# Attention 1 of a two-layer kernel: transposed probabilities by head, values in two passes

## What is computed

```
q, k, v = (x @ W.T).reshape(B, T, 16, 16).transpose(0, 2, 1, 3)   # for Wq, Wk, Wv
scores = einsum('bhqd,bhkd->bhqk', q, k) * 16 ** -0.5, causal mask
attn = softmax(scores)
out = einsum('bhqk,bhkd->bhqd', attn, v).reshape(B, T, 256) @ Wo.T
```

## Time and profile before

| what | us |
|---|---|
| median of three runs | 939.19 |
| lowest and highest run | 936.19, 939.78 |
| the profiled execution, its own time | 939.04 |
| its span, first to last instruction | 937.1 |
| TensorE busy over the span | 863.4 (92%) |
| VectorE busy | 616.3 (66%) |
| ScalarE busy | 567.0 (61%) |
| GpSimd busy | 456.4 (49%) |
| the first attention, from its first matmul to its end | 19.4 to about 178 |

### The profile page before, as it was taken

One profiled execution on the slowest core, in us unless ns is written; L12 is line 12 of the kernel. 1 busy time (PEld: TensorE's weight loads), 2 busy tenths in 40 slices (PEclk: granted clock), 3 DMA queues, 4 the chain that ended last, 5 costly groups with the idle time before them and its releaser, 6 DMA issues. The chain is left out here.

```text
span 937.1 us, 18767 instructions
## 1 busy us (share of the span) xinstructions
PE 863.4 (92%) x6108; PEld 799.0 (85%) x6108; DVE 616.3 (66%) x1620; ACT 567.0 (61%) x1570; POOL 456.4 (49%) x486
## 2 busy tenths in 40 slices
PE   5799997769999999999999999969999999999994
PEld 4699987668989989999889999858888888888884
DVE  5466768667787788877887777664545545454456
ACT  6889888656767776667676676654334343333333
POOL 3734334277677776677677777610222212222121
PEclk9999999998999999999999999997999999999997
DMA  7000000051124111411111111101433333333321
GB/s 238 1 22 27 22 23 1 23 147 35 34 61 122 47 40 40 136 46 45 36 35 46 45 37 47 41 1 41 150 107 102 116 117 100 112 101 117 118 79 45
DMA packets 50246, 63.34 MB, mean 68 GB/s; under 512 B 5728, under 2 KB 36064, under 8 KB 50176
## 3 DMA queue, kind: packets, MB, share of 16 engines
q1 hardware_dynamic: 49088, 61.41, 22.4%
q10 hardware_dynamic: 1088, 1.05, 0.3%
HBM read 41.86 MB, written 1.18 MB: 46 GB/s over the span
## 5 line engine op out<-in xcount | busy, mean ns | idle before, releaser
L639 POOL TENSOR_TENSOR b_prob<-b_prob,b_rsum 128x256 f32<-128x256 f32 (+1 forms) x128 | 104.8, 840 | 104.3 <-DVE b_rsum L621 104.3
L73 PE MATMUL banks<-act_t,b_w 128*128 128x256 f32 (+1 forms) x392 | 129.5, 330 | 4.4 <-DVE b_work L1203 3.3
L74 PE MATMUL banks<-act_t,b_w 128*128 128x256 f32 (+1 forms) x392 | 127.4, 325 | 0.0
L75 PE MATMUL banks<-act_t,b_w 128*128 128x256 f32 (+1 forms) x392 | 127.1, 324 | 0.0
L1965 ACT ACTIVATE moe_hid<-banks 128x512 fp32r<-128x512 f32 x66 | 39.5, 598 | 124.6 <-DVE banks L2056 124.6
L1364 ACT ACTIVATE b_prob<-banks,b_negmax 128x128 f32<-128x128 f32 (+1 forms) x256 | 103.6, 416 | 12.6 <-DVE b_negmax L1351 12.5
L2049 DVE TENSOR_TENSOR moe_gated<-banks,moe_share 128x512 f32<-128x512 f32 x66 | 45.6, 691 | 85.1 <-PE banks L75 81.2
L1220 ACT ACTIVATE b_qt<-b_work 128x512 fp32r<-128x512 f32 x64 | 40.5, 632 | 97.5 <-POOL b_work L1215 97.5
L1215 POOL TENSOR_TENSOR b_work<-b_work 128x512 f32<-128x512 f32 x64 | 88.1, 1377 | 9.2
L639 POOL TENSOR_TENSOR a_prob<-a_prob,a_rsum 128x256 f32<-128x256 f32 x64 | 52.4, 840 | 75.5 <-DVE a_rsum L621 75.3
L1211 POOL TENSOR_TENSOR b_work<-b_work,rope_t 128x512 f32<-128x512 f32 x64 | 83.2, 1299 | 7.2 <-DMA b_work<-b_work 7.2
(11 more groups left out here) (237 smaller groups left out, 3019.1 us busy)
## 6 DMA issues: line engine op xcount, KB each, us to landing
b_work<-b_work SPq DMA_DIRECT2D x128, 128.0 KB, 2.3
moe_share<-gates SPq DMA_DIRECT2D x32, 512.0 KB, 3.6
b_w_raw<-in_b_wq SPq DMA_DIRECT2D x4, 1024.0 KB, 5.5
b_w_raw<-in_b_wo SPq DMA_DIRECT2D x4, 1024.0 KB, 9.0
a_src_t<-act_t SPq DMA_DIRECT2D x5, 512.0 KB, 3.0
moe_w_raw<-in_wg SPq DMA_DIRECT2D x16, 128.0 KB, 2.1
moe_w_raw<-in_wu SPq DMA_DIRECT2D x16, 128.0 KB, 2.2
moe_w_raw<-in_wd SPq DMA_DIRECT2D x16, 128.0 KB, 2.2
```

The source lines that it names most:

```text
L73: nc.tensor.matmul(out, w_lo, m_hi, start=start, stop=False, skip_group_check=skip)
L74: nc.tensor.matmul(out, w_hi, m_lo, start=False, stop=False, skip_group_check=skip)
L75: return nc.tensor.matmul(out, w_hi, m_hi, start=False, stop=stop, skip_group_check=skip)
L639: last = self.m.nc.gpsimd.tensor_tensor(rows, rows, rsum[:, :, t:t + 1].to_broadcast([PART, 2, width]), ALU.mult)
```

## The change

`AttentionA` gets its own versions of four steps and of VectorE's slot.

- **A bank for each head.** Head h's three turned blocks (384 columns, `PCOLS`) lie in one bank of its own. TensorE waits for the low part of the same head of the pair before, turns three blocks, and signals; then it does the same for the other head. The semaphores count heads (`TURNS = 2`).
- **Copied and subtracted by head.** ScalarE makes two copies of 384 columns in place of one of 768, each after its head's turns. VectorE makes two subtractions of 384.
- **By turns.** VectorE's order is maxima of head 0, low part of head 0, maxima of head 1, low part of head 1; then as before.
- **Values in two passes.** A head's block of 128 values' columns holds its high part in 16 columns and its low part in the 16 beside them. One pass over the low and one over the high part of the probabilities does all products: 8 matmuls a pair in place of 12. Four heads fill 128 partitions, so the iteration's output takes 512 columns in place of 256 (two groups, `VG`). The blocks `self.v` need half the room, and GpSimd clears half.
- **Output.** The copy and the subtraction of the output take 512 columns in place of 256. The projection does 12 matmuls in place of 6: two groups, each with weights `wo` in which every head's 16 rows stand twice (for the high and the low part).
- **Weights spread.** At the start of the stage SP issues 16 DMAs from SBUF to SBUF that write the rows of Wo into `wo`, ahead of its first source copy. TensorE waits for them once, before the values of the last pair of iteration 0.

```diff
 class AttentionA(Attention):
+    TURNS = 2
+    def turned(self, h):
+        return self.m.pt_ps[:, 2 * h * SEQ:2 * h * SEQ + PCOLS]
+    def pe_prob_t(self, pe, p, P):
+        wait(pe, self.prob_ready, P + 1)
+        for h in range(2):
+            wait(pe, self.pt_ready, 2 * P - 1 + h)
+            for k in range(PCOLS // PART):
+                last = nc.tensor.transpose(self.turned(h)[:, k * PART:(k + 1) * PART],
+                                           self.prob[:, p, h, k * PART:(k + 1) * PART], m.ident[:])
+            last.then_inc(self.pt_full, 1)
+    def act_prob_t(self, act, p, P):
+        wait(act, self.pv_done, P - 1)
+        for h in range(2):
+            wait(act, self.pt_full, 2 * P + 1 + h)
+            self.m.nc.scalar.activation(self.prob_t_of(p, 0, h), self.turned(h),
+                                        ACT.Copy).then_inc(self.pt_hi, 1)
+    def dve_prob_t(self, dve, p, P, h):
+        wait(dve, self.pt_hi, 2 * P + 1 + h)
+        self.m.nc.vector.tensor_tensor(self.prob_t_of(p, 1, h), self.turned(h),
+                                       self.prob_t_of(p, 0, h).bitcast(F32),
+                                       ALU.subtract).then_inc(self.pt_ready, 1)
+    def slot_dve(self, dve, it, p, units=True):
+        now, prob = self.stage(it, p, 0), self.stage(it, p, 3)
+        for h in range(2):
+            if now:
+                self.dve_max(dve, *now[1:], heads=(h,))
+            if prob:
+                self.dve_prob_t(dve, *prob[1:], h)
...
-        self.v = place(2 * NTT * HPI * PART, "p (a t h n) -> p a t h n", a=2, t=NTT, h=HPI)
+        self.v = place(NTT * HPI * PART, "p (t h n) -> p t h n", t=NTT, h=HPI)
-        self.ot = sb("ot", [PART, 2, SEQ], F32R)
+        self.ot = sb("ot", [PART, 2, VG * SEQ], F32R)
+        self.wo = place(2 * NC * VG * D, "p (a c g n) -> p a c g n", a=2, c=NC, g=VG)
...
     def pe_values(self, pe, it, p, P):
-        wait(pe, self.pt_ready, P + 1)
+        if isinstance(it, int) and it == 0 and p == PAIRS - 1:
+            wait(pe, self.wo_spread, 16 * SPREADS)
         for h in range(2):
             head = 2 * p + h
+            wait(pe, self.pt_ready, 2 * P + 1 + h)
             for k in range(NTT):
-                last = three(nc, m.o_ps[:, k * PART:SEQ],
-                             self.v[:, 0, k, head, :], self.v[:, 1, k, head, :],
-                             self.prob_t[:, par, 0, at:at + width], self.prob_t[:, par, 1, at:at + width],
-                             head == 0 and k == 0, head == HPI - 1 and k == NTT - 1)
+                for part in (1, 0):
+                    last = nc.tensor.matmul(m.o_ps[:, g * SEQ + k * PART:(g + 1) * SEQ], self.v[:, k, head, :],
+                                            self.prob_t[:, par, part, at:at + width],
...
+    def sp_spread(self, sp):
+        src = self.m.a_wo[:].rearrange("p (a c n) -> p a c n", a=2, c=NC).bitcast(F32)
+        for g in range(VG):
+            for h in range(VH):
+                of = (g * VH + h) * A_DH
+                for part in range(2):
+                    to = (2 * h + part) * A_DH
+                    sp.dma_start(self.wo[to:to + A_DH, :, :, g, :].bitcast(F32), src[of:of + A_DH, :, :, :],
+                                 ).then_inc(self.wo_spread, 16)
...
     def pe_project(self, pe, it, p, P):
         for t in range(NTT):
-            last = three(nc, m.y_ps[:, t * D:(t + 1) * D],
-                         self.ot[:, 0, t * PART:(t + 1) * PART], self.ot[:, 1, t * PART:(t + 1) * PART],
-                         m.a_wo[:, bass.ds(at, D)], m.a_wo[:, bass.ds(at + NC * D, D)], True, True)
+            for g in range(VG):
+                o = lambda part: self.ot[:, part, g * SEQ + t * PART:g * SEQ + (t + 1) * PART]
+                last = three(nc, m.y_ps[:, t * D:(t + 1) * D], o(0), o(1), self.wo_at(it, 0, g),
+                             self.wo_at(it, 1, g), g == 0, g == VG - 1)
...
-        self.m.nc.scalar.activation(self.ot[:, 0, :], self.m.o_ps[:, 0:SEQ],
+        self.m.nc.scalar.activation(self.ot[:, 0, :], self.m.o_ps[:],
-        self.m.nc.vector.tensor_tensor(self.ot[:, 1, :], self.m.o_ps[:, 0:SEQ],
+        self.m.nc.vector.tensor_tensor(self.ot[:, 1, :], self.m.o_ps[:],
...
         def _(sp):
+            self.sp_spread(sp)
```

More of the change, by code:

```diff
@@ L318, in _ @@
             nc.gpsimd.memset(m.q_stack[:, 0:NTT * HPI * PART].bitcast(F32), 0.0)
-            k_at = 2 * B_W + 2 * NTT * HPI * PART
+            k_at = 2 * B_W + NTT * HPI * PART
             nc.gpsimd.memset(m.b_w[:, k_at:k_at + NTT * HPI * STACK].bitcast(F32), 0.0)
@@ L423 @@
     LATE_NEXT = False
+    TURNS = 1
     POOL_NORMALISES = False
@@ L566, in act_exp @@
         nc, m = self.m.nc, self.m
-        wait(act, self.pt_full, P - PAIRS + 1)
+        wait(act, self.pt_full, self.TURNS * (P - PAIRS + 1))
         for h in range(2):
@@ L603, in slot_act, with dve_max @@
             self.act_weights(act, it)
-    def dve_max(self, dve, p, P):
+    def dve_max(self, dve, p, P, heads=(0, 1)):
         nc, m = self.m.nc, self.m
         wait(dve, self.exp_done, 2 * P - 2)
-        for h in range(2):
+        for h in heads:
             wait(dve, self.s_full, 2 * P + 1 + h)
@@ L705, in run, with prob_t_of @@
                 after(k)
+VH, VG, SPREADS = 4, 2, 16
 class AttentionA(Attention):
+    TURNS = 2
+    def turned(self, h):
+        return self.m.pt_ps[:, 2 * h * SEQ:2 * h * SEQ + PCOLS]
+    def prob_t_of(self, p, part, h):
+        return self.prob_t[:, p % 2, part, h * PCOLS:(h + 1) * PCOLS]
+    def pe_prob_t(self, pe, p, P):
+        nc, m = self.m.nc, self.m
+        wait(pe, self.prob_ready, P + 1)
[23 more added lines that the diff above has]
+                self.dve_prob_t(dve, *prob[1:], h)
+        if before := self.stage(it, p, 1):
+            self.dve_normalise(dve, *before[1:])
+        if out := self.stage(it, p, 4):
+            self.dve_outputs(dve, *out)
+        u = self.early_unit(p, units)
+        if u is not None:
+            self.dve_unit(dve, it + 1, u)
+        if now and p == PAIRS - 1:
+            self.dve_values(dve, it)
+        if p == 0 and not (isinstance(it, int) and it < 2):
+            self.dve_add(dve, it - 2)
     ITS, UNITS = A_ITS, 4
@@ L834, in pe_values, with wo_at @@
             head = 2 * p + h
+            wait(pe, self.pt_ready, 2 * P + 1 + h)
             for k in range(NTT):
                 width = SEQ - k * PART
-                at = h * SEQ if k == 0 else 2 * SEQ + h * PART
-                last = three(nc, m.o_ps[:, k * PART:SEQ],
-                             self.v[:, 0, k, head, :], self.v[:, 1, k, head, :],
-                             self.prob_t[:, par, 0, at:at + width], self.prob_t[:, par, 1, at:at + width],
-                             head == 0 and k == 0, head == HPI - 1 and k == NTT - 1)
-        last.then_inc(self.pv_done, 1)
+                at = h * PCOLS + k * SEQ
+                g = head // VH
+                for part in (1, 0):
+                    last = nc.tensor.matmul(m.o_ps[:, g * SEQ + k * PART:(g + 1) * SEQ], self.v[:, k, head, :],
+                                            self.prob_t[:, par, part, at:at + width],
+                                            start=head == 0 and k == 0 and part == 1,
+                                            stop=head == HPI - 1 and k == NTT - 1 and part == 0,
+                                            skip_group_check=True)
+        last.then_inc(self.pv_done, 1)
+    def wo_at(self, it, part, g):
+        flat = self.wo.rearrange("p a c g n -> p (a c g n)")
+        return flat[:, bass.ds((it % 2) * (VG * D) + (part * NC * VG + g) * D, D)]
+    def sp_spread(self, sp):
[7 more added lines that the diff above has]
+                                 ).then_inc(self.wo_spread, 16)
     def pe_project(self, pe, it, p, P):
@@ L877, in v_view @@
     def v_view(self, part, t):
-        base = self.v[:, part, t, 0, 0:A_DH]
+        base = self.v[:, t, 0, part * A_DH:(part + 1) * A_DH]
         return bass.AP(tensor=base.tensor, offset=base.offset,
-                       ap=[list(base.ap[0]), [PART + A_DH, HPI], [1, A_DH]])
+                       ap=[list(base.ap[0]), [VH * PART, VG], [PART + 2 * A_DH, VH], [1, A_DH]])
     def act_values(self, act, it):
@@ L888, in act_values @@
         for t in range(NTT):
-            row = self.values(it, t).rearrange("p (h d) -> p h d", h=HPI)
+            row = self.values(it, t).rearrange("p (g h d) -> p g h d", g=VG, h=VH)
             last = nc.scalar.activation(self.v_view(0, t), row, ACT.Copy)
@@ L973, in _ @@
             sp.wait_ge(self.src_loaded, 16 * (self.ITS - self.COPIED))
+            sp.wait_ge(self.wo_spread, 16 * SPREADS)
         @block.gpsimd
```

4 lines of the change are left out of this document (2 added, 2 removed).

## The result

The changed kernel takes 941.09 us (median of 20 runs, 936.26 to 948.45) against 938.5 for the kernel before (20 runs too): a ratio of 1.0037, 95% interval [1.0023, 1.0052], so 3.5 us slower (2.2 to 4.9); the medians themselves lie 2.6 apart. The profiled execution took 943.26 us.

A forecast was written before the change was run, and what follows sets the result against it. TensorE, busy all 16.47 us of an iteration, and an equally long chain through ScalarE and VectorE bound it. 5 × 0.49 − 5 × 0.09 − 0.46 − 0.13 + 1.5 = +2.9 us on 939.04 gave 942, range 936 to 947.

The forecast's parts named there:

- Slot 3 to the end of unit 0: First attention's loop: wider output and longer projection make it 8.41 us against 7.92, +0.49, five times; TensorE idle 0.70.
- Rival 1: First attention: TensorE alone decides, so the whole −9.1 us shows and the kernel takes 930; chance 0.10.
- end of unit 0 to slot 3: First attention's loop: paced exponentials +0.21, VectorE +0.08, turns −0.33, hand-over −0.05, so −0.09 us, five times.
- The pacing of the second exponentials: First attention: the second head's exponentials wait for VectorE's second maximum, starting 1.65 us after the maxima instead of 1.44: +0.21.
- slots 4 to 8: Iteration ahead of the steady loop: only slot 4 gains, −0.46 us for values without projection and −0.13 at its start.
- the loop's second chain: Through ScalarE's and VectorE's stacks, sum, maxima, exponentials, low part and turns, end of unit 0 to slot 3: 8.54 us.
- The tail: First attention's last slots: VectorE's pace, copies, paced exponentials and longer projections, less the drain's gain, make +1.5 us.
- the drain by heads: Last slots: turning, copying and subtracting by head shortens each link; with the last values −1.6 us before the last output's copy.
- There fewer matmuls give nothing: Tail, where VectorE works 14.96 of 15.14 us and TensorE waits for its low part: removing matmuls has no effect.
- Rival 2: First attention: each switch on VectorE costs up to 0.17 us, 37 of them 6.3, giving 948; chance 0.18.
- Rival 3: First attention: the two banks free nothing, so the −0.33 us falls away five times and in the drain: 945; chance 0.07.
- Rival 4: First attention's tail and front gain more from the drain by heads and early turns: 2 to 5 us less, 938; chance 0.15.

The follow-up runs named there:

- Experiment 3: Changed kernel with the second four heads' output left out (copy and subtraction of 256 columns, projection of 6 matmuls): 935.22 us, 0.9964 to the kernel before.
- experiment 6: Kernel before with a bank per head, copies and subtractions by head and VectorE's turns, but three values passes and the short output: 937.63 us, ratio 1.0001.
- Experiment 10: Changed kernel with four unused matmuls put into slots 25 to 35 and also ahead of the projections in slots 28, 32 and 36: 938.61 us, ratio 1.0012.
- maxima first: Changed kernel with VectorE taking both heads' maxima, then both low parts: 942.28 us, ratio 1.0045 to the kernel before.
- two passes only: Changed kernel with the old layout, copies, subtraction and order of the turned probabilities, keeping the values in two passes: 943.25 us, ratio 1.0046 to the kernel before.
- the changed kernel again: Changed kernel, unaltered, run once more: 942.34 us, ratio 1.0044 to the kernel before.
- experiment 8: Changed kernel with four unused matmuls put into slots 25 to 35 except slots 28 and 32: 939.82 us, ratio 1.0006 to the kernel before.
- experiments 2 and 4: Two separate edits of the changed kernel: both maxima ahead of both low parts, 942.28 us (1.0045); unit 0 ahead of the projection in slot 0, 937.81 us (0.9991).
- 12: Changed kernel with unit 0 ahead of the projection, filling matmuls in the tail and ahead of its projections, and both maxima first: 933.97 us, ratio 0.9962.
- experiment 11: Changed kernel with unit 0 ahead of the projection and filling matmuls in the tail and ahead of its projections: 936.25 us, ratio 0.9986.

## Why the prediction was right, and where by luck

The forecast of 942 stands beside 941.09, and the direction and size of the ratio fit (2.9 us forecast, 3.5 measured). Step by step it was less good than that.

**Shown right: where the saving goes.** Slot 3 to the end of unit 0 was forecast at 8.41 us and took 8.39; the projection at 4.88 started at 4.90; TensorE, ready at 4.18, loses 0.72 (0.2 ahead of slot 0's second scores, the rest ahead of the projection). Experiment 3 takes the wider output away and gets 0.8 us an iteration. Rival 1 (TensorE alone decides, 930) fell: TensorE's weight loads fell from 16.03 to 14.91 us an iteration, and the iteration grew. The Trainium skill, "Perfetto Trace Analysis", section "Identifying the Most-Contended Engine", says to optimize the engine with the highest occupancy first, which was TensorE; it doesn't say how much of a saving there will show, and that the whole of it would was my reading.

**A term mis-sized: end of unit 0 to slot 3.** −0.09 forecast, −0.20 measured (8.34 for 8.54). The pacing of the second exponentials is there in full (0.99 for 0.79), but the stacks followed at 0.81 where I had 0.88, and the turns started 0.05 us after the low part's end, where I had 0.10 (0.15 before). So an iteration is 16.7, not 16.87.

**A term mis-sized: slots 4 to 8.** −0.59 forecast with slot 4's start, 16.44 to 15.03 = −1.4 measured. I gave slots 5 to 7 nothing, taking the loop's second chain for granted. They gave 1.09 (11.48 to 10.39), most of the 3 × 0.46 that fewer matmuls save; slot 4 gave 0.32 (4.96 to 4.64). VectorE has no sum to add in that iteration (0.60 in the loop), so the chain is shorter there and TensorE sets most of the pace. Slots 1 to 4, also at nothing in my sum, gave 0.14 (10.79 to 10.65).

**The tail: right at full clock.** +2.0 with slot 24's 0.49; measured piece by piece where the clock stayed up, it is 1.23 (slots 24 to 28: 21.53 for 20.30) + 0.05 (to slot 31: 14.06 for 14.01) + 0.43 (to the end: 19.13 for 18.70) = 1.7. From slot 31 on, the drain by heads and the open last projection nearly cancel, as forecast; in experiment 6, which has the first without the second, that piece took 17.88.

**The step that failed: "There fewer matmuls give nothing".** In the tail TensorE waits for VectorE, and I took matmuls removed there as free of effect. They aren't: in all seven profiles with two passes and no filling, the clock fell between slot 24 and the second attention, in none of the three with three passes. A fall costs 0.8 us at 145 (14.83 for 14.06 in slots 28 to 31) and 1.4 to 1.5 at 164 or 167 (from slot 31 on 20.65 and 20.52 for 19.13), since the now longer projection lies in it. So from slot 1 on the stage is not +2.9 but −1.5 (slots 1 to 8) + 0.9 + 1.7 = +1.1 at full clock, and 1.9 to 2.6 with one fall. (Slot 0 and what comes ahead of it are left out: they took 11.0 to 12.5 us, in the three profiles of the changed kernel alone 11.1, 11.3 and 12.4.) Experiment 10 bears this out, changed work and full clock all through the stage: 147.2 us from slot 1 to the second attention for 146.1 in the first profile of before, and 1.0012 in the whole, which is +1.1 us too. The other 1 to 3 us of the three measured differences (3.5, 4.1 and 5.3) are not in the stage; they must lie behind it, where I had forecast nothing.

**Luck.** The sum came out near because errors of opposite sign met: the loop (+1.6 forecast, +0.9 measured) and the slots 1 to 8 (−0.6 forecast, −1.5 measured) are too high in it by 1.6 us, and the clock, inside the stage and behind it, is missing with 2 to 4.

**The other rivals.** Rival 2 (switches on VectorE) did not decide: the starts lie 0.53 and 0.47 apart without a gap. Rival 3 fell (three turns lie ahead of the second low part). Rival 4's gain in the front was there (slots 4 to 8), but not 2 to 5 us in all.

**What stays open.** How much of the difference lies behind the stage, and why. That filling the tail makes the whole kernel faster is shown (1.0056 to 1.0012 on one chip). That a fall in the tail brings falls in the experts, 450 us later, is only suggested: four of the seven unfilled kernels with two passes have one at 658 to 672 us, but maxima first, two passes only and the changed kernel again have falls in the tail and none there, and so has experiment 8. Nor is one profile the mean of its kernel: experiment 6, with three passes, was profiled at 936.8 us and a mean granted clock of 0.98, but 4 of its 12 executions took 940.3 to 941.8 us at 0.969 to 0.974, as low as the changed kernel's (0.964 to 0.980). Filling was never tried on the kernel before, and neither were the edits of experiments 2 and 4. So it isn't shown either that 12 is faster by the change: unit 0 and the maxima first might serve the old kernel as well.

## What to carry to other kernels

A busy engine with no hole can be one of two chains of equal length: follow the second one through the other engines before pricing work taken off the first, and ask which operand of the next step the removal makes wider. Put a unit of independent work where TensorE waits for an output to be copied and split, rather than behind it (16.7 to 16.15 us an iteration here). And where matmuls are removed in a stretch in which TensorE waits for others, look at the granted clock of that stretch: useless matmuls in the waits were worth 3 to 4 us in the changed kernel, but nothing that the runs can tell once unit 0 was moved.

## What the runs showed of the hardware

- Removing matmuls from a stretch bound by VectorE brought TensorE from its higher clock level to the lower one for stretches of 3 to 4 us (granted 0.50; one of 6.8), in 7 profiles of 7, and in none of 3 without the removal. No single wait of TensorE there was long: in the changed kernel's first profile the longest that its rows show between 120 and 176 us was 1.24 us (1.45 in the kernel before, where the clock stayed up). With four short matmuls a slot put back, 3 profiles of 4 show no such stretch up to the change of stage, and the fourth (experiment 8) shows one, from a wait that was not filled. At the change of stage, with a wait of 2.34 us, kernels of both kinds fall: experiment 11 at 175.0 us, 0.3 ahead of the second attention's first matmul, the kernel before and that with only the banks at 179.2 and 177.8, 1.2 to 1.3 behind it.
- A stretch at the lower level between 658 and 672 us, in the experts, came in 4 of the 7 unfilled kernels with two passes and in none of the 7 others. These four took 762.4 to 764.8 us behind the stage, the ten others 756.6 to 759.5, with identical instructions.
- VectorE subtracting from one bank while TensorE writes the other cost nothing that the rows show: a subtraction of 384 columns took 0.55 us beside turns (117.99, with turns at 117.71) and without them (113.26).
